# MLP of a Swin block on one core: GpSimd makes the low half of the GELU of the second bank

## The reference

```python
def _ln(x, g, b):
    m = jnp.mean(x, -1, keepdims=True)
    v = jnp.mean(jnp.square(x - m), -1, keepdims=True)
    return (x - m) / jnp.sqrt(v + EPS) * g + b
...
x1 = shortcut + out                      # out: the attention's result
h = _ln(x1, norm2_g, norm2_b)
h = jax.nn.gelu(h @ fc1_w + fc1_b, approximate=False)
h = h @ fc2_w + fc2_b
return x1 + h
```

## Time and profile before

| | us |
|---|---|
| median of 3 runs | 1015.25 |
| lowest and highest | 1012.13, 1016.6 |
| the profiled execution's own time | 1012.1 |
| its span | 1010.3 |
| of it, MLP phase | about 802.5 to 1010.3 |
| of that, steps at an even pace | 829 to 990 |

### The profile page before, as it was taken

One profiled execution on the slowest core, in us unless ns is written; L12 is line 12 of the kernel. 1 busy time (PEld: TensorE's weight loads), 2 busy tenths in 40 slices (PEclk: granted clock), 3 DMA queues, 4 the chain that ended last, 5 costly groups with the idle time before them and its releaser, 6 DMA issues. The chain is left out here.

```text
span 1010.3 us, 45295 instructions
## 1 busy us (share of the span) xinstructions
PE 935.3 (93%) x16004; PEld 752.3 (74%) x16004; DVE 897.6 (89%) x2029; ACT 763.1 (76%) x1734; POOL 782.2 (77%) x971
## 2 busy tenths in 40 slices
PE   1489999999999999999999999999998489999998
PEld 0258888888888888888888888888887346666665
DVE  5668999999999999999999999999996599999997
ACT  0368888888888888888888888888886445555554
POOL 6348888888888888888888888888886667776772
PEclk9999999999999999999999999999999689999999
DMA  2023332222222222222222223222222045555554
GB/s 58 12 70 77 79 79 66 68 76 77 76 66 68 77 76 76 66 70 76 76 75 66 70 76 76 74 67 72 75 67 58 1 90 116 118 114 118 119 111 109
DMA packets 139237, 77.32 MB, mean 77 GB/s; under 512 B 105923, under 2 KB 138980, under 8 KB 139190
## 3 DMA queue, kind: packets, MB, share of 16 engines
q1 hardware_dynamic: 139190, 76.69, 30.9%
HBM read 10.48 MB, written 9.63 MB: 20 GB/s over the span
## 5 line engine op out<-in xcount | busy, mean ns | idle before, releaser
L415 POOL TENSOR_TENSOR pl<-p 113x294 f16<-113x294 f32 x512 | 347.8, 691 | 53.5 <-ACT p L486 42.5
L811 DVE TENSOR_REDUCE rowmax<-banks 113x12 f32<-113x588 f32 x256 | 192.4, 752 | 46.2 <-PE banks L634 45.9
L651 PE MATMUL banks<-Qh,KAg 128*128 128x147 f16 x2048 | 218.1, 228 | 0.0
L486 ACT ACTIVATE p<-banks 113x294 f32<-113x294 f32 x512 | 207.1, 418 | 11.6 <-PE banks L651 7.7
L651 PEld LDWEIGHTS banks<-Qh,KAg 128*128 128x128 f16 x2048 | 166.7, 97 | 31.2
L667 PE MATMUL banks<-Vb,p 113*128 113x36 f16 x3072 | 183.7, 180 | 0.9 <-POOL pl L415 0.9
L667 PE MATMUL banks<-Vb,pl 113*128 113x36 f16 x1536 | 169.2, 180 | 0.0
L667 PEld LDWEIGHTS banks<-Vb,p 113*128 113x128 bf16 x3072 | 161.9, 97 | 1.1 <-POOL pl L415 1.1
L1041 ACT ACTIVATE gel<-banks 128x448 f32<-128x448 f32 (+1 forms) x192 | 91.2, 511 | 88.0 <-PE banks L1073 86.5
L620 PE MATMUL banks<-bs_h,idt 113*128 113x294 f16 x512 | 146.6, 294 | 10.4 <-DVE rowmax L811 2.4
L620 PE MATMUL banks<-bt_h,idt 113*128 113x294 f16 x512 | 148.3, 290 | 2.5 <-DMA Qh<-mT 1.9
(11 more groups left out here) (150 smaller groups left out, 2688.4 us busy)
## 6 DMA issues: line engine op xcount, KB each, us to landing
Qh<-QAB SPq DMA_DIRECT2D x192, 98.0 KB, 2.2
Vb<-Vn SPq DMA_DIRECT2D x256, 54.0 KB, 2.1
xres<-in_x SPq DMA_DIRECT2D x64, 147.0 KB, 2.2
KAh<-KA SPq DMA_DIRECT2D x192, 49.0 KB, 1.9
out_y<-ybuf SPq DMA_DIRECT2D x64, 147.0 KB, 2.1
Qh<-mT SPq DMA_DIRECT2D x128, 4.6 KB, 2.2
hT<-htok SPq DMA_TRANSPOSE x48, 2.8
w<-in_weights SPq DMA_DIRECT2D x1, 278.9 KB
```

The source lines that it names most:

```text
L415: nc.gpsimd.tensor_tensor(pl[p % 4][:, :, :, 0:N].rearrange("p a w n -> p (a w) n"), p32[p % 4][:, :, :, 0:N].rearrange("p a w n -> p (a w ...
L486: nc.scalar.activation(p32[p % 4][:, :, :, 0:N].rearrange("p a w n -> p w a n"), src, ACT.Exp, scale=1.0 / SB).then_inc(s_exp, 1)
L651: i = nc.tensor.matmul(bank[:, w * COLS:(w + 1) * COLS], KAg[upar][:, 2 * p + w, :, :].rearrange("p g n -> p (g n)"), Qh[upar][:, level, : ...
L811: nc.vector.tensor_reduce(rowmax[:, 2 * p:2 * p + 4, :].rearrange("p (k w) a -> p k (w a)", k=2), sc[0:AP_, :, 0:2 * COLS].rearrange("p k ...
```

## The change

POOL gets a third operation in step t, after `xc` and `mxn`: the low part of the second bank's GELU (split 1), with a semaphore of its own, `s_gl1`. DVE no longer does it. PE waits for both semaphores before fc2.

```diff
+        s_gl1 = sem("gelu_low_of_second_bank_ready")
...
@@ the GpSimd step, after mxn
+                if exists(t):
+                    pool.wait_ge(s_g, 3 * t + 2)
+                    nc.gpsimd.tensor_tensor(gl[par][:, 1, 0:3 * PT], gel[par][:, 1, 0:3 * PT], g_high(par)[:, 1, 0:3 * PT],
+                                            ALU.subtract).then_inc(s_gl1, 1)
...
@@ the TensorE step, before fc2
-                    pe.wait_ge(s_gl, 3 * t)
+                    pe.wait_ge(s_gl1, t)
+                    pe.wait_ge(s_gl, 2 * t)
...
@@ the VectorE step
                 def split(k):
                     dve.wait_ge(s_g, 3 * t + k + 1)
-                    cols = 3 * PT if k == 1 else HTOK
-                    nc.vector.tensor_tensor(gl[par][:, k, 0:cols], gel[par][:, k, 0:cols], g_high(par)[:, k, 0:cols],
+                    nc.vector.tensor_tensor(gl[par][:, k, 0:HTOK], gel[par][:, k, 0:HTOK], g_high(par)[:, k, 0:HTOK],
                                             ALU.subtract).then_inc(s_gl, 1)
...
-                if exists(t):
-                    split(1)
                 if exists(t):
                     split(2)
```

## The result

The changed kernel takes 1030.17 us (median of 4 runs, 1026.32 to 1031.7), the one before 1014.27 (4 runs, 1012.13 to 1016.6). The ratio is 1.0159, with a 95% interval of 1.0139 to 1.0179: 16 us slower. The prediction was 1034, within 1020 to 1041.

The account below looks back on a forecast made before the run. The bound was taken to be what DVE and POOL share, a chain of 3.02 us a step. It would grow to 3.35; 0.33 over 56 steps adds 18.5 us to 1015.25, giving 1034, range 1020 to 1041.

Parts of the forecast that it names:

- What bounds the kernel: MLP even stretch: DVE and POOL instructions reading SBUF exclude each other; one chain of handovers sums to 3.02 us a step.
- the 14.4 us of the earlier trace: Ahead of fc2 in the MLP's even stretch: PE was said to wait for a split 37 times, 14.4 us in all.
- PE's pace as the next bound: fc1 and fc2 on PE: 2.88 us a step would come next, so 0.14 a step could be won.
- The new split's own time: POOL's split of 336 columns: 0.78 us, scaled from the attention's `pl`; low end 0.74; 0.64 in the chain.
- Two places for three POOL instructions: DVE lets POOL in at two places a step, so `mxn` and the new split go back to back; `mxn` costs 0.72.
- The sum: MLP chain after the change: 3.35 a step, 0.33 more, times 56 steps is 18.5 us; 1034 on the median.
- The 1037 given for the highest run's base: Upper end of the likeliest times, 1029 to 1037, taken from the highest run as base.
- Who waits: PE idles 0.47 a step ahead of fc2 for POOL's split; DVE idles before split 0; the split's GELU wait is free.
- rival 4: Worse than forecast: PE gets a lower clock, or one more handover a step is lost; 8 us, 1042; chance 0.07.
- Rival 1: Waiting POOL instruction let in between mlo and split 2: 3.18 a step, 9 us more, 1024; chance 0.25.
- Rivals 2 and 3: 2: POOL's split hidden, 8 us less, 1007, chance 0.05; 3: a wash, 1015 give or take 5, chance 0.08.

## Why the prediction was right, and where it was off

- **What bounds the kernel** (the shared chain, 3.02): right. Removing 0.42 of it gave PE's pace, and so did leaving DVE its work and taking one input out of SBUF. One reading beside it was wrong: the 14.4 us of the earlier trace rows are waits of the weight load (PEld). PE itself idled 1.9 us in those 161, so they are not the difference between 3.02 and PE's pace; where that shows on PE stays open.
- **PE's pace as the next bound**: the term was 2.88 from the earlier trace rows; measured 2.92, since one step in four takes 0.15 more (there is one such step in each turn of the loop). So the removal could bring 0.10 a step, not 0.14.
- **The new split's own time**: 0.78 by the columns of `pl`; measured 0.74, the low end. In the chain that is 0.62 instead of 0.64.
- **Two places for three POOL instructions**: right. In the changed kernel's timeline POOL waited with an instruction while mlo ended and split 2 was next in 58 steps, and DVE kept its turn in all 58; at the end of split 0 POOL was let in ahead of mlo in all 57. Not foreseen: in 12 steps `xc` and `mxn` make the pair, mlo lasts 1.76 us, and the new split waits behind split 2. The sum is 3.30 there too.
- **The sum**: 0.29 a step (0.287 unrounded) instead of 0.33, times 56 is 16.1 us instead of 18.5; measured 15.9 in the MLP. The mis-sized terms are small: the new split (0.62 for 0.64), split 0 (0.46 for 0.48) and `mxn` (0.71 for 0.72) were too long, `xc` (0.62 for 0.61) too short; mlo and split 2 were right. Of the 3.8 us by which the median lies under 1034, 2.6 are this sum, 1.0 is the base, 1015.25 then and 1014.27 now, and the rest is rounding. That the profiled execution's 1030.4 meets the 1030.6 worked out for it is luck, with 2.4 us from the attention in it. The 1037 given for the highest run's base is a slip: 1016.6 + 18.5 is 1035.1.
- **Who waits**: right in kind. POOL's split waits for its GELU 0.1 us in all, DVE idles 0.2 to 0.6 ahead of split 0 in about three steps of four (not in the steps of the other order), and PE waits for POOL's split in 42 of 49 steps. PE's idle time was overestimated: 161.00 less 145.81 is 15.2 us, 0.31 a step instead of 0.47. The clock stayed at 1.00, so the part of rival 4 that rested on it fell.
- **Rival 1** (1024, POOL let in between mlo and split 2) fell: it happened in none of the 58 steps, and the median lies 6 us above it. The Trainium skill, "SBUF — State Buffer", section "Who interferes with whom", says that a VectorE instruction with two SBUF inputs contends with a GpSimd instruction that reads SBUF and not with one that only writes it. The runs agree: split 0 took its 0.62 beside the memset. The same section of the Trainium skill says that a VectorE instruction with at most one SBUF input, outside the 2-port modes, does not contend with GpSimd. The runs agree here too: split 2 took 0.61 beside `mxn`. It says as well that the order of issue decides who blocks; the 58 steps, in which split 2 was started after POOL's waiting instruction and went first, speak against it.
- **Rivals 2 and 3** fell with the pace of 3.31, and so did the lost handover of rival 4.

**What stays open**: what decides who is let in. Not the kind of the second instruction (3.30 with the other kind), and not first come, first served. DVE can pass POOL with two instructions. With the two splits next to each other, POOL's split, started behind DVE's waiting second split, went first in 13 of 27 steps and not in the other 14.

## What to carry to other kernels

Where instructions of two engines exclude each other, the two engines are one resource: a split moved from VectorE to GpSimd took more of the shared time there (0.62 instead of 0.42, and `mxn` went from 0.61 to 0.71 beside it), so such a move can help only if the shared time isn't what binds. Before moving work, compare one instruction's duration where the other engine is busy with that where it is idle; if the longer one ends a fixed time after the other engine's end, the sum over both engines is the bound. The cure here was in the operands: one input from PSUM instead of SBUF, paid with idle time of ScalarE, gave back all of the loss and some 5 us more.

## What the runs showed of the hardware that I had not expected

- A VectorE subtraction of 128x448 with its float32 input in PSUM and its bf16 one in SBUF takes 0.61 us, as with both in SBUF, and does not block GpSimd.
- The order of arrival does not decide in every case: behind mlo DVE kept its turn 58 times of 58, with POOL waiting longer, while behind split 0 it gave it up 57 times of 57; and `mxn` passed a waiting mlo in 12 steps of the changed kernel where it had yielded in 41 others of the same order.
- A memset of 768 float32 columns on GpSimd takes 0.73 us and left VectorE's split, with two SBUF inputs, at its 0.62.
